# A graph layer on one Trainium2 core: row degrees known strip by strip, or quarter by quarter

## The reference

```
A = adj + eye(8192)
deg = sum(A, axis=1)
d = rsqrt(deg)
h = (A * d[:, None] * d[None, :]) @ x
y = x + elu(h @ w)
out = (y - mean(y)) / sqrt(var(y) + 1e-5)      # over the 128 columns
```

## Time and profile before

| | us |
|---|---|
| median of 3 runs | 1055.69 |
| lowest, highest | 1055.21, 1061.57 |
| profiled execution | 1055.05 |
| its span, first to last instruction | 1053.3 |

### The profile page before, as it was taken

The page is one execution under the profiler, slowest core; times in us unless marked ns, Lnnn a source line. Parts: engine busy times, 40 slices in busy tenths (PEclk is TensorE's granted clock), DMA queues, the critical chain, the costliest instruction groups (busy, mean ns, idle before and its releaser), DMA issues. The chain is left out here.

```text
span 1053.3 us, 35548 instructions
## 1 busy us (share of the span) xinstructions
PE 923.3 (88%) x16000; PEld 831.4 (79%) x16000; DVE 763.8 (73%) x633; ACT 703.6 (67%) x1677; POOL 194.3 (18%) x267
## 2 busy tenths in 40 slices
PE   0089399399797998999999999999999999999995
PEld 0065288287797898899998997999999999999994
DVE  0496497576587667868788767997988797866933
ACT  6898798898888898898989989862214715031201
POOL 0120120210401304040412433466001101000000
PEclk9999689799899899999999999999999999999998
DMA  9999999999999999999999999989998898899920
GB/s 385 401 387 413 399 393 402 396 400 396 399 394 387 379 387 393 336 391 392 392 395 394 385 396 389 357 272 311 376 304 277 284 326 290 303 304 309 352 80 21
DMA packets 168809, 367.28 MB, mean 349 GB/s; under 512 B 6224, under 2 KB 32976, under 8 KB 158416
## 3 DMA queue, kind: packets, MB, share of 16 engines
q1 hardware_dynamic: 151616, 356.54, 91.4%
q10 hardware_dynamic: 17040, 8.46, 2.8%
HBM read 360.78 MB, written 4.19 MB: 347 GB/s over the span
## 5 line engine op out<-in xcount | busy, mean ns | idle before, releaser
L892 PE MATMUL p_set<-space 32*128 32x256 f32 (+3 forms) x15872 | 906.9, 386 | 117.6 <-ACT space L800 56.1
L892 PEld LDWEIGHTS p_set<-space 32*128 32x128 f32 x15872 | 816.0, 188 | 204.1 <-issue 132.3
L910 DVE STREAM_TRANSPOSE space<-space 128x2048 f32<-128x2048 f32 x256 | 579.5, 2292 | 113.6 <-ACT space L792 86.2
L792 ACT ACTIVATE space<-space 128x512 f32<-128x512 f32 (+2 forms) x744 | 578.8, 779 | 83.4 <-DMA space<-in_adj 76.4
L934 DVE TENSOR_TENSOR hT<-p_set,hT 128x1024 f32<-128x1024 f32 (+2 forms) x109 | 105.9, 991 | 118.6 <-PE p_set L892 118.6
L792 ACT ACTIVATION_READ_ACCUMULATOR space<-space 128x1 f32 x744 | 138.8, 187 | 0.0
L815 ACT ACTIVATE space<-space 128x512 f32<-128x512 f32 x16 | 10.1, 631 | 181.5 <-DVE space L945 181.3
L775 POOL COPY space<-xn 32x512 f32<-32x512 f32 x192 | 120.0, 625 | 12.3
L759 POOL TENSOR_TENSOR d<-deg,half 128x4 f32<-128x4 f32 x16 | 16.3, 1017 | 541.7 <-DVE deg L916 541.7
L800 ACT ACTIVATE space<-xn 32x512 f32<-32x512 f32 x96 | 60.2, 627 | 47.8 <-POOL xn L765 38.9
L782 POOL TENSOR_TENSOR rstd<-var_eps,half 128x4 f32<-128x4 f32 x16 | 16.5, 1031 | 239.0 <-DVE var_eps L979 239.0
(11 more groups left out here) (16 smaller groups left out, 28.8 us busy)
## 6 DMA issues: line engine op xcount, KB each, us to landing
space<-in_adj SPq DMA_DIRECT2D x332, 1024.0 KB, 12.2
xn<-in_x SPq DMA_DIRECT2D x20, 256.0 KB, 11.2
space<-in_x ACTq DMA_DIRECT2D x16, 256.0 KB, 7.2
out_rows<-space ACTq DMA_DIRECT2D x16, 256.0 KB, 7.1
space<-in_adj SPq DMA_DIRECT2D x4, 768.0 KB, 12.3
ident<-in_w ACTq DMA_DIRECT2D x1, 64.0 KB, 5.3
```

The lines of the kernel that those rows point to most:

```text
L792: ins = nc.scalar.activation(view[:, g], view[:, g], ACT.Copy, accum_out=to[:, g:g + 1])
L892: ins = nc.tensor.matmul(to, xs_chunk(h, j)[quadrant(q)], moving, start=first and s == b == 0, stop=last and s == b == 3)
L910: nc.vector.transpose(slots[slot], slots[slot]).then_inc(tile_turned, 1)
```

## The change

For the strips 2 to 11 (`HALVED`), the kept blocks are read in four pieces of 128 rows (`PIECES`). First come the far reads, then the first quarter of every kept block of the strip, then x of the band ("split"), then the second, third and fourth quarter of all of them ("rest"), with nothing between these. For the quarters after the first a group may need semaphores of its own (`rest_loaded`). The degrees, the power, the scaling of x and each of its 16 copies are done for each quarter by itself, with 128 columns in place of 512 (four times as many instructions on DVE, POOL and ACT). `deg` keeps two buffers.

PE may open a job for the already turned kept blocks of a band of which the first quarter is known (at least two, at most four, evenly spaced), when no whole job is ready and a product set is free. It multiplies the quarter of each block that meets that quarter of x: 4 x 4 of the job's 4 x 4 x 4 matmuls. The set stays with the job until its fourth quarter. At most two such jobs are open (`HALF_JOBS`). A whole job of such a band waits for all four quarters' copies.

KEPT changes for bands 11 to 15, from 4, 1, 2, 3, 4 to 2, 3, 4, 4, 2; it adds up to 58, so 78 blocks are read twice. The planner's costs of a quarter's operations are added.

```diff
-KEPT = (1, 2, 3, 4, 5, 6, 5, 4, 4, 4, 5, 4, 1, 2, 3, 4)
+KEPT = (1, 2, 3, 4, 5, 6, 5, 4, 4, 4, 5, 2, 3, 4, 4, 2)
+HALVED = range(2, 12)
+HALF_JOBS = 2
+PIECES = 4
...
+def halves_of(r):
+    return tuple(range(PIECES)) if r in HALVED else (None,)
...
+    return items + near + [("split", r), ("rest", r)]
...
+        slot, some, group = take_slot(("tile", len(tiles))), [], len(groups)
+        nk = BLOCKS // PIECES
+        return first_piece([("near", r, nk * j, nk, t, 1, slot, j, group) for j in range(PIECES)])
...
+    def first_piece(these):
+        if these[0][1] not in HALVED:
+            return these
+        many = BLOCKS // PIECES
+        rest.extend(v for v in these if v[2] >= many)
+        return [v for v in these if v[2] < many]
...
+        if row_todo and row_todo[0][0] == "split":
+            row_todo.pop(0)
+            pending_x.append(at_row)
+        if row_todo and row_todo[0][0] == "rest":
+            row_todo.pop(0)
+            queued.extend(sorted(rest, key=lambda v: v[2] // (BLOCKS // PIECES)))
+            rest.clear()
...
+        for n, (job, home, these, piece) in enumerate(half_jobs):
+            if piece in usable[home]:
+                half_jobs[n] = (job, home, these, piece + 1)
+                if piece == PIECES - 1:
+                    half_jobs.pop(n)
+                parts.append((job, home, these, False, piece == PIECES - 1, piece))
+                return len(parts) - 1
...
+            for t in HALVED:
+                if len(half_jobs) >= HALF_JOBS or t not in home_of or 0 not in usable.get(home_of[t], ()) or whole(t):
+                    continue
+                some = [i for i in turned_early if tiles[i][:2] == ("first", t)]
+                these = next((c for m in range(min(MERGE, len(some)), 1, -1) for c in map(in_steps, combinations(some[:8], m)) if c), [])
...
-                    r = arg
-                    pool.wait_ge(row_summed, row_nth[r])
-                    nc.gpsimd.tensor_tensor(d[:, r], deg[:, r % 2], half[:, :], ALU.pow).then_inc(d_ready, 1)
+                    r, half = arg
+                    blocks = blocks_of(half)
+                    pool.wait_ge(row_summed, row_nth[arg])
+                    nc.gpsimd.tensor_tensor(d[:, r, blocks], deg[:, r % 2, blocks], minus_half[:, blocks], ALU.pow).then_inc(d_ready, 1)
...
-                        nc.gpsimd.tensor_copy(xs_part(h, q, s), xn[quadrant(s), h % XN]).then_inc(copied_by["pool"], 1)
+                        nc.gpsimd.tensor_copy(xs_part(h, half, q, s), x_part(h, half, s)).then_inc(copied_by["pool"], 1)
...
-                    for b in range(BLOCKS):
+                    for b in range(BLOCKS)[blocks_of(half)]:
```

More of the change, by code:

```diff
@@ L252, in issue, with end_row @@
             in_flight += 1
+            share = load[3] * load[5] * (BAND if load[0] == "near" else 1) / 2048 if load[0] != "tile" else 1.0
             wide = load[5] * (BAND if load[0] == "near" else 1) if load[0] != "tile" else BAND
[L254 removed]
+            dma = max(dma, now + 1.0) + share * (FAR if wide == 2048 else MID if wide >= 1024 else NEAR)
             events.append((dma + LAND, k, "landed", k))
[L256 to L265, removed]
+            if not row_todo and not queued:
+                end_row()
+    def end_row():
+        nonlocal at_row, row_todo, rows_done, backlog
+        if rows_done or any(f[1] == at_row for f in firsts):
+            return
+        open_band(at_row)
+        if at_row not in HALVED:
+            pending_x.append(at_row)
+        backlog += sum(1 for v in tiles if v[0] == "first" and v[1] == at_row)
+        if at_row + 1 < BANDS:
+            at_row += 1
+            row_todo = strip_items(at_row, kept)
+        else:
+            rows_done = True
+            close_stage()
     def close_stage():
@@ L274, in close_stage, with row_summed, whole @@
                 release(slot)
[L276 to L279, removed]
+    def row_summed(load):
+        r = load[3] if load[0] == "tile" else load[1]
+        k0, nk = (0, BLOCKS) if load[0] == "tile" else load[2:4]
+        for half in halves_of(r):
+            many = BLOCKS if half is None else BLOCKS // PIECES
+            base = many * half if half is not None else 0
+            rows = len(set(range(k0, k0 + nk)) & set(range(base, base + many)))
+            wide = 1 if load[0] == "tile" else load[5] if load[0] == "near" else load[5] // BAND
+            if rows:
+                sums_left[r, half] -= rows * wide
+                if not sums_left[r, half]:
+                    offer("dve", 0, "row_sum", (r, half), 0.35)
+    def whole(t):
+        return t in home_of and len(usable.get(home_of[t], ())) == len(halves_of_home(home_of[t]))
     def tile_summed(i):
@@ L558, in gcn_resnorm, with sums_for @@
             summed_rows[load[3] if load[0] == "tile" else load[1]].append(k)
+    def sums_for(r, half):
+        blocks = blocks_of(half)
+        return [k for k in summed_rows[r] if loads[k][0] == "tile" or loads[k][2] < blocks.stop and loads[k][2] + loads[k][3] > blocks.start]
     adds, begun = [], {}
@@ L872, in _ @@
                     continue
-                job, h, these, first, last = parts[arg]
+                job, h, these, first, last, half = parts[arg]
                 bank, rows, _ = jobs[job]
```

210 lines of the change are left out of this document (132 added, 78 removed).

## The result

The changed kernel takes 1058.6 us (median of 22 runs, 1056.68 to 1062.45) against 1055.87 us (22 runs) for the kernel before: 0.22% more, ratio 1.0022, interval 1.0013 to 1.0030. 1050 us was forecast, a gain of 0.5%. It stayed within the 1% that was called no change, and moved the other way.

A forecast was written before the change was run, and what follows sets the result against it. PE was taken as the bound, waiting for strips' degrees until 596.82 us; 7.2 us recovered in transfers less 2.3 us of longer toll at strip 9 gave 4.9 us, 1055.05 - 4.9 = 1050 us, range 1039 to 1064.

The forecast's parts named there:

- The lead: PE, strips 2 to 5: early quarters win 6, 2, 7 and 7 us, leaving PE some 7 us ahead after strip 5.
- I take all 7.2 as recovered: SP's transfers, strips 4 to 9: PE's lead frees slots earlier and wins back the lost 7.2 us (ends 0 and 7.2).
- The toll: Strip's degrees to PE at full pace: strip 9 goes from 6.75 to 9.1 us, a loss of 2.3 us.
- The early work: PE before x is complete: one pair, 5.25 us, in strips 2, 3, 7, 8, 9; two, 10.5 us, in 4, 5, 6, 10.
- The first pair's pacing: PE at a strip's start: POOL's copies pace the first pair, 9.75 us instead of 7.0, so 2.75 us are lost.
- The rule that strips 8 and 9 decide: PE's lead of some 7 us must pass strips 8 and 9, where PE is already just in time (gap 0.79 us).
- PE's own work: PE: matmuls as many and as wide as before, so its work is unchanged at 7.0 us a pair.
- KEPT's new bands: Late bands: repeats fall from 79 blocks to 78, 2.7 us of transfers where PE is the bound; worth nothing.
- The x load ahead of the last quarters: SP's queue: costs nothing in strip 9; in strip 10 a 9 us wait, covered by some 12 us of issued transfers.
- 1.2 us early: Landing of a strip's last degrees: +0.65 us for x ahead of them, -1.85 us for a shorter last sum, so -1.2.
- B: Slower rival, POOL: copies hardly shrink; a quarter over 6.1 us eats the whole 7.2; at 9 us, 1074 us. Chance 0.1.
- C: No-change rival, PE: early jobs hold both product sets 14.7 us, or slots go sooner, using up the lead; 1056 us. Chance 0.18.

The follow-up runs named there:

- second profile: The changed kernel run and profiled again with no edit: 1058.74 us, ratio 1.0026 to the kernel before; this profile spans 1057.0 us.
- before_less5: Kernel before, stages s = 1 and 2 left out of two products of band 5 (7 us of PE's work, wrong results): 1055.82 us, ratio 0.9996.
- kept_only: Kernel before with only the new KEPT of bands 11 to 15, no strip in quarters: 1057.82 us, ratio 1.0008.
- after_short: Changed kernel without POOL's four copies of stage s = 1 in all bands, PE reading the s = 0 chunk (wrong results): 1054.67 us, ratio 0.9992.
- before_lessall: Kernel before, stages s = 1 and 2 left out of all first products of bands 2 to 9 (wrong results): 1047.48 us, ratio 0.9918.
- experiment 5: POOL's s = 1 copies left out: changed kernel, all bands 0.9992, from 7 1.0007, to 6 1.0009; kernel before 0.9995.
- short_hi: Changed kernel without POOL's four copies of stage s = 1 in bands 7 and later alone (wrong results): 1057.19 us, ratio 1.0007.
- short_lo: Changed kernel without POOL's four copies of stage s = 1 in bands up to 6 alone (wrong results): 1056.75 us, ratio 1.0009.
- before_pow2: Kernel before with a second power on POOL ahead of each of the 16, into a spare tile, x 1.0 us later: 1062.23 us, ratio 1.0058.
- q_oldkept: Quarters alone, with KEPT as in the kernel before: 1058.15 us, ratio 1.0023 to the kernel before.
- after_noact: Changed kernel with ACT's two copies of each quarter done by DVE instead: 1064.36 us, ratio 1.0071 to the kernel before.

## Why the prediction was wrong

*The lead.* Right: 6, 2, 7 and 7 us were forecast for strips 2 to 5; when the first products of each of these bands end, the second profile is ahead of the kernel before by 6.6 (264.5 against 271.1), 1.1, 5.2 and 7.0 us, from fewer and shorter gaps. In the midst of strip 2, at 40 blocks, it was 1.9.

*The step that failed* is "I take all 7.2 as recovered". Strip 9's degrees came 1.0 to 1.9 us earlier (588.4 and 587.5 us), where the sum needed 7.2, and those of strips 6 to 8 came within 0.5 us of their old dates (457.8, 505.3 and 548.8 us against 457.3, 505.4 and 549.2). The working put PE's lead beside the waits of SP and took every wait shorter than the lead as gone. But PE came early to degrees that were not early: it was done with band 6 at 506.3 us, the last degrees of strip 7 were known at 505.3 and all of its x was there only at 517.4 (516.3 before). Its first two pairs there took from 506.1 to 525.1 us, 19.0 us for 14.0 us of work, with waits of 0.70 and 1.64 us and, in the second profile, a granted clock of 0.76 from 512 to 518 us. The kernel before came to strip 7 at 511.5 us and didn't wait at all. The bounds had 0 as an end, and the value was taken at the other. How much of the 7.2 us was had went with how long the lead lasted: 0.1 us at strip 9 in before_less5, where it died at strip 6, 3.8 in kept_only, 4.5 in after_short, 7.8 in before_lessall. That is one profile of each.

*The toll*, the time from a strip's degrees to PE at full pace. A quarter costs POOL somewhat more than forecast: the copy was put at 0.23 us and is 0.291, the power at 1.10 from start to start and is 0.63 (0.552 and its gap), the scale at 0.40 with its gap and is 0.40 without. That is 5.3 us (0.63 + 0.46 + 4.2), not 4.9, and a strip 21. For strip 9 x was to be complete 14.3 us after the old date, and is 16.0 after it (605.43 against 589.45). The early work was mis-sized the other way. The prediction gave strips 3, 7, 8 and 9 one early pair each; the planner opens two there, at strip 9 the blocks (9,6) with (9,7) and (9,8) with (9,10), the last of them a block of the next strip. (In strip 10 it opens one instead of two, in strip 5 one job of four blocks.) PE's row has 168 instructions from 595.37 us to 605.00, before x is complete: 9.2 us of work at 7.0 us a pair, where 5.25 were forecast. So the toll at strip 9 is 16.0 - 9.2 = 6.8 us, as in the kernel before, and not the 9.1 of the prediction. The backlog agrees: 135.3 against 134.8 at 136 blocks. That strip 9 would cost 2.3 us more than before was wrong; that the kernel ended 2.7 us slower, near the 2.3 that the prediction's sum gives with nothing recovered, is a coincidence.

*The first pair's pacing*, 2.75 us of the toll, was put down to POOL's copies. In strips 2 to 4, from which the prediction took it, it was PE's clock (rows in experiment 5).

*The rule that strips 8 and 9 decide.* Not borne out: short_hi and short_lo give about half each, and before_pow2 shows a delay piling up from strip to strip (0.9 us at strip 5, 3.7 at 7, 3.9 at 9).

*What was costed at nothing.* PE's own work: its busy time is 923.3 us before, 922.6 in kept_only, and 934.9 and 936.9 us in the two profiles of the changed kernel. Most of the difference lies in strips 2 and 3, in stretches at the lower clock that stand where PE had waited, so it isn't all time lost. KEPT's new bands, "nothing" since PE is the bound in the last stage: their order makes PE wait 1.4 to 2.0 us for an add at 857 us, and the last stage is 2.3 us longer in the second profile, where 152 blocks were reached with a backlog only 0.6 us above the old one. The medians of kept_only (1.0008, unclear) don't prove a cost of it by itself, and q_oldkept loses 1.0023 without it. The x load ahead of the last quarters cost nothing visible at strip 9, and strip 11's degrees came 5 us later (653.3 against 648.3); in q_oldkept it was 6.8, in kept_only 2.1. Whether SP's wait for POOL's copies did that wasn't tried. Strip 3's and 4's degrees came 4 us late, where 1.2 us early was forecast; after_noact rules out ACT's copies as the only cause, and it stays open what the rest is.

*The rivals.* B had the right engine and the wrong place. POOL's quarters at 5.3 us are under its 6.1, and strip 9 itself lost next to nothing; but with a third of POOL's copies left out the change's loss is gone (after_short), so POOL's longer chain is what the change pays, spread over the strips. By which waits it comes to be paid at the end isn't shown in full. C, product sets held by two early jobs, shows in no wait of PE for an add longer than 0.3 us in the second profile, those ahead of output products left aside, and wasn't tested by itself.

## What to carry to other kernels

Before a lead on one engine is booked as time won, ask what sets the next date: take that engine's work away in one place, and everywhere, and look at the dates alone. A wait in a queue's list (here 476.6 us of SP behind PE) is time to be won only as far as the queue ran dry, which was 8 us here, and a lead that meets x before its date wins none of it. Being late is dearer: 1.0 us in each strip cost 6. And cutting a serial chain into four multiplies its fixed costs: 10.2 us of POOL became 21, and the change was slower by 2.7 us until a third of the copies were left out. When an engine's first work after a long wait is slow, look at its clock before blaming the engine that feeds it.

## What the hardware showed that was not expected

- Small operations on POOL: a copy of 32x128 takes 0.291 us and one of 32x512 0.626; the power 0.552 us for one column and 1.02 for four; the scale 0.400 for 128x128 and 1.04 for 128x512. On ACT a 32x128 copy takes 0.307 us, on DVE 0.244.
- PE's early quarters ran partly at the lower of its two clock levels. Stages of 8 instructions took 1.24 us each at strip 2 and 0.71 at strip 4 (rows above), and 1.24 at strip 3 (first row below). In the changed kernel from 265 to 280 us the granted clock was 0.58 on average (0.66 in the second profile), after PE had stood 3.40 us with short stretches behind it; a granted clock of 0.5 is 1.2 GHz. So the filling of a gap in small pieces took longer than its instruction counts say, there. The columns of the second row are as in experiment 5.

```profile
271.26 1.24 PE L1016 MATMUL p_set<-space 32*128 32x256 f32 x8 [0.18 <-POOL space L899]
...
265.00:280.00 15.00, 10.46 (x80) 5.80 (x80) 10.64 (x15) 13.51 (x44) 11.96 (x38) 0.58 1.05 392
```
